# Cross-attention and mixture-of-experts block on one core: the rows are routed without being normalised first

## The chip, the cores and the metric

The kernel runs on one core of one Trainium2 chip. The metric is the device time of one execution in microseconds; the median of three executions is given. The profile is one further execution of the same program, with times counted from the start of its span. Engines are named as in the profile: PE is TensorE, DVE is VectorE, ACT is ScalarE, POOL is GpSimd, SP is SyncE; PEld is TensorE's weight load, and a "q" behind an engine's name (SPq, ACTq) is a DMA that it issues.

## The reference, cut to what matters

```python
# x: (16, 112, 256) = 1792 rows of 256; ctx: (16, 375, 256)
x = x + xattn(layernorm(x), ctx, ctx, mask, Wq, bq, Wk, bk, Wv, bv, Wo, bo)   # 16 heads of 16
x = x + ffn(layernorm(x), router_w, w1, w2)

def ffn(flat, router_w, w1, w2):                  # flat: (1792, 256), router_w: (256, 8)
    gate_probs = softmax(flat @ router_w)
    topk_w, topk_idx = top_k(gate_probs, 2)
    topk_w = topk_w / clip(topk_w.sum(-1), 1e-9)
    cw = zeros(T, 8).at[arange(T)[:, None], topk_idx].add(topk_w)
    h = silu(einsum('td,edf->etf', flat, w1))     # 8 experts, 256 -> 512 -> 256
    y = einsum('etf,efd->etd', h, w2)
    return einsum('etd,te->td', y, cw)
```

`layernorm` takes the mean off a row and divides by the root of its variance plus 1e-5.

## The kernel before

The program has three phases. A prologue loads and transposes x, projects the queries of all 16 batches and fills the first keys and values. Then come 16 turns, one for each batch (`turn(b)`, L1725 on PE): scores and their maxima for the next batch (`head_scores`, the maxima on DVE at L1105), transposed scores (`quad_scores`, L1626), exponentials on ACT (`exps`, L834), outputs (`quad_outputs`, L1640), and the projections of a later batch (`product`, L1546). The third phase is the experts: 21 steps of 256 gathered rows (`step(t)`), from about 299 us to the end.

Between the second and the third lies the routing. The 1792 rows are 14 tiles of 128. `UNITS` (L64) groups them: six units of two tiles and, last, units 6 and 7 of one tile each. For each unit u:

- `project_output(u)` on PE makes the attention's projection, `residual(u)` on DVE (L1231) adds x and the bias and leaves the sum in `x2`;
- `row_vars(u)` on DVE (L1238, L1245, L1247) makes mean and variance, `roots(u)` on POOL (L715) the inverse root, and `normalise_rows(u)` on POOL (L723, units 0 to 5) or `normalise_late(u)` on DVE (L1284, units 6 and 7) writes the normalised rows to `xn2`;
- `write_rows(u)` on SP (L546) copies them to `xn_rows` in DRAM, from which the experts gather them;
- `flat_transpose(u)` on PE (L1709) transposes `xn2` into PSUM, `flat_high(u)` on ACT (L942) copies it out as the high part, `flat_low(u)` on DVE (L1290) makes the low part, and `route(u)` on PE (L1719, L1721) multiplies: a tile takes four matmuls, two for each half of the 256 columns;
- `read_logits(u)` on DVE (L1296) adds the two halves of the result into `logits`.

When the logits of the first eight tiles are there, `find_two(early_tiles, 4)` on DVE (L1315 to L1324) finds the two best experts of each row; `rank_early` on PE counts, `place_rows(0)` on DVE (L1347 to L1353) makes each row's place, ACT makes the one-hot places (`places_in_block`, L972 and L976), POOL and DVE the lanes (L731, L1359). The same follows for the last six tiles (`find_two(late_tiles, 8)`, `rank_late`, L1866 to L1872, `place_rows(1)`, `places_in_block(TOP, ...)`). `fill_lanes` (L1880) and `list_rows` on PE and `list_tokens` on DVE (L1396, L1397) then make the list by which POOL gathers the rows (L765). `gather_rows` waits for that list and for all eight copies to DRAM. PE runs `spin` (L1907), matmuls whose results nobody reads, until the first rows are there.

The order on every engine is written out by hand: an engine runs its list in that order, and a wait holds all that stands behind it. On PE the attention of the last batch and the routing of the first units are interleaved. On SP the two loads of the experts' weights (L552 and L557, 4 MB each) stand between the copies of the rows.

Of the kernel before, what the change touches and what calls it, by code (L numbers as in the profile page):

```python
# [5 lines left out]
F32 = mybir.dt.float32  # L6
F32R = mybir.dt.float32r
# [59 lines left out]
BK_FLAT = (3, 5, 3, 5, 1, 2, 3, 5)  # L67
BK_RANK, BK_LATE, BK_PLACED, BK_TOKEN = 4, 6, 7, 0
# [37 lines left out]
def xattn_moe_kernel(nc, x_rows, x_tiles, ctx_t, mask, wq_t, wk_t, wv_t, wo_t, bq, bk, bv, bo,  # L106
                     router_w, w1, w2, out):
    ctx = ExitStack()
    with ctx:
# [27 lines left out]
        rw = sb("router_parts", [P, KD, 2 * E], F32R)  # L137
# [42 lines left out]
        def expert_buffers(p):  # L180
# [113 lines left out]
        cursor["at"] = last_query_at  # L294
        fh = [sb(f"flat_t_hi{p}", [P, KD, TG], F32R) for p in range(2)]
        fl = [sb(f"flat_t_lo{p}", [P, KD, TG], F32R) for p in range(2)]
# [43 lines left out]
        wh_ready, wl_ready, rw_ready = (sem(n) for n in (  # L340
            "wh_ready", "wl_ready", "rw_ready"))
        ch_ready, cl_ready = (sem(n) for n in ("ch_ready", "cl_ready"))
        keep_in = [sem(f"keep_in{p}") for p in range(2)]
        mask_in, first_low_stacked, masked_set, mask_rows_ready, mask_written = (sem(n) for n in (
            "mask_in", "first_low_stacked", "masked_set", "mask_rows_ready", "mask_written"))
# [22 lines left out]
        ft_done, fh_ready, fl_ready, logits_done = (sem(n) for n in (  # L368
            "ft_done", "fh_ready", "fl_ready", "logits_done"))
# [40 lines left out]
        def stack_part(queue, b, c, src, done):  # L410
            for a in range(2):
# [3 lines left out]
                                src[half:half + P // 2, b.n // 2, b.n % 2, :, :].bitcast(F32)).then_inc(done, 16)  # L415

# [5 lines left out]
        def _(sp):  # L422
# [117 lines left out]
            def write_rows(u):  # L540
                if u < 6:
                    sp.wait_ge(early_xn_ready, u + 1)
                else:
                    sp.wait_ge(late_xn_ready, u - 5)
                tiles = tiles_of(u)
                sp.dma_start(xn_rows[1 + P * tiles.start:1 + P * tiles.stop, :].rearrange("(n p) d -> p n d", p=P),  # L546
                             xn2[u % XN_RINGS][:, 0:UNITS[u][1], :]).then_inc(xn_written[u % XN_RINGS], 16)
# [11 lines left out]
            for u in range(6, 8):  # L559
                write_rows(u)  # L560

# [18 lines left out]
        def _(pool):  # L580
# [26 lines left out]
            def keep_rows():  # L607
                pool.wait_ge(mask_in, 16)
                pool.wait_ge(zeros_set, 1)
                pool.tensor_scalar(masked[:, :], m_all[:, :], 0.0, None, ALU.is_equal).then_inc(masked_set, 1)  # L610
                pool.wait_ge(masked_set, 1)
# [173 lines left out]
        def _(act):  # L785
# [1262 lines left out]
```

## Time and profile before

| what | us |
|---|---|
| median of 3 runs | 452.66 (452.36 to 453.35) |
| the profiled execution, its own time | 451.87 |
| its span | 449.9 |
| PE busy | 411.5 (91%) |
| DVE busy | 336.4 (75%) |
| ACT busy | 279.8 (62%) |
| POOL busy | 223.9 (50%) |
| mean granted TensorE clock | 0.959 of full speed |

The profiled execution lies 0.8 us under the median of the runs. A busy PE is not a PE at its peak, since matmuls overlap: the time that one costs is the distance from its start to the start of the next. The granted clock has two levels, 2.4 GHz (1.00) and 1.2 GHz (0.50).

### The profile page before, as it was taken

What the parts mean: (1) busy time and instruction counts of PE and PEld (TensorE: products, weight loads), DVE (VectorE), ACT (ScalarE), POOL (GpSimd) and SP (SyncE); (2) the same over time, 40 slices, a digit from 0 to 9 for tenths busy, and PEclk for the clock granted to TensorE, in tenths of its full rate; (3) what the DMA queues carried; (4) which work ended last, traced back from release to release, by engine and by line L of the source; (5) the groups of instructions that cost most, each with busy time, mean ns of one, the idle gap of its engine ahead of it and who ended that gap; (6) DMA issues with size and microseconds to landing.
All of it is one profiled execution on the core that took longest, in us unless ns stands there. A gap on an engine that the chain in (4) does not pass through costs nothing.

```text
span 449.9 us, 10827 instructions
## 1 busy us (share of the span) xinstructions
PE 411.5 (91%) x4219; PEld 382.5 (85%) x4219; DVE 336.4 (75%) x700; ACT 279.8 (62%) x381; POOL 223.9 (50%) x257
## 2 busy tenths in 40 slices
PE   7878999999999999999999996899999999999910
PEld 6747898999989999999998985789999999999910
DVE  7866778778877888787788778856886667776536
ACT  4767476665566665766555554648778777778600
POOL 6757443312444223433202764675787878876420
PEclk9999999999999999999999997589999999999975
DMA  7995676768866778766450259822222322332169
GB/s 213 237 199 155 135 158 131 150 150 162 197 159 156 153 140 189 157 132 128 96 120 3 75 205 365 272 68 73 85 80 85 95 83 94 83 82 73 47 231 306
DMA packets 44675, 64.32 MB, mean 143 GB/s; under 512 B 6801, under 2 KB 33570, under 8 KB 44626
## 3 DMA queue, kind: packets, MB, share of 16 engines
q1 hardware_dynamic: 38322, 50.40, 45.6%
q0 software_dynamic: 4096, 11.13, 8.2%
q10 hardware_dynamic: 2208, 2.12, 1.4%
q8 instruction: 33, 0.54, 0.5%
q14 instruction: 16, 0.13, 0.1%
HBM read 30.13 MB, written 9.28 MB: 88 GB/s over the span
## 4 chain that ended last, share of the span: by engine, by line
PE 79%; DVE 9%; DMA 5%; ACT 3%; issue 2%; POOL 1%; ACTq 0%; SPq 0%; DVEq 0%
PE ps L1546 41%; PE ps L1609 12%; PE ps L1626 9%; PE ps L1640 9%; PE ps L1915 2%; DVE x L1536 2%; PE ps L1653 2%; DMA q_stack<-attn_t_lo 1%; DMA y_back<-y_rows 1%; DVE neg_max L1105 1%; DMA keep<-keep_scratch 1%; PE ps L1709 1%; DMA keep_scratch<-keep_all 1%; PE ps L1665 1%; PE ps L1719 1%
## 5 line engine op out<-in xcount | busy, mean ns | idle before, releaser
L1105 DVE TENSOR_REDUCE neg_max<-ps 112x1 f32<-112x376 f32 x256 | 133.6, 545 | 41.4 <-PE ps L1609 36.5
L834 ACT ACTIVATE probs<-ps 125x1344 f32<-125x1344 f32 x64 | 82.8, 1294 | 43.4 <-PE ps L1626 38.2
L1609 PE MATMUL ps<-k_stack,q_stack 98*112 98x376 f32 x256 | 86.2, 369 | 3.7 <-DVE neg_max L1105 2.2
L604 POOL TENSOR_TENSOR k_lo<-k_f,k_hi 128x752 fp32r<-128x752 f32 x16 | 28.9, 1806 | 112.3 <-ACT k_hi L808 111.8
L765 POOL DMA_INDIRECT rows<-xn_rows,token_of_row x42 | 55.8, 1328 | 17.5 <-issue 12.5
L773 POOL DMA_INDIRECT y_rows<-y_out,slot_of_row x42 | 45.6, 1087 | 25.3 <-ACT y_out L1027 14.4
L1609 PEld LDWEIGHTS ps<-k_stack,q_stack 98*112 98x112 f32 x256 | 44.1, 174 | 16.3 <-DVE neg_max L1105 10.9
L1626 PE MATMUL ps<-q_stack,k_stack 100*125 100x224 f32 x384 | 52.6, 273 | 0.0
L1626 PEld LDWEIGHTS ps<-q_stack,k_stack 100*125 100x125 f32 x384 | 50.4, 188 | 0.7 <-ACT probs L834 0.5
L1546 PE MATMUL ps<-w_hi,h_hi 128*128 128x256 f32 x168 | 48.8, 290 | 0.4 <-DVE h_lo L1452 0.4
L1546 PE MATMUL ps<-flat_t_hi,w_hi 128*128 128x256 f32 x168 | 47.5, 283 | 1.3 <-DVE flat_t_lo L1430 1.3
L1546 PE MATMUL ps<-flat_t_hi,w_lo 128*128 128x256 f32 x168 | 47.2, 281 | 0.0
L1546 PE MATMUL ps<-flat_t_lo,w_hi 128*128 128x256 f32 x168 | 47.2, 281 | 0.0
L1546 PE MATMUL ps<-w_hi,h_lo 128*128 128x256 f32 x168 | 47.0, 280 | 0.0
L1546 PE MATMUL ps<-w_lo,h_hi 128*128 128x256 f32 x168 | 47.0, 280 | 0.0
L1640 PE MATMUL ps<-probs,v_wide 125*32 125x112 f32 x1536 | 47.0, 262 | 0.0
L1640 PEld LDWEIGHTS ps<-probs,v_wide 125*32 125x32 f32 x1536 | 35.1, 109 | 8.0 <-issue 5.7
L1008 ACT ACTIVATE h_f<-ps 128x1024 f32<-128x1024 f32 x21 | 21.6, 1026 | 24.3 <-PE ps L1546 24.3
L1546 PEld LDWEIGHTS ps<-flat_t_hi,w_hi 128*128 128x128 f32 x168 | 31.9, 190 | 1.7 <-DVE flat_t_lo L1430 1.7
L1546 PEld LDWEIGHTS ps<-w_hi,h_hi 128*128 128x128 f32 x168 | 31.9, 190 | 0.9 <-DVE h_lo L1452 0.9
L1452 DVE TENSOR_TENSOR h_lo<-h_f,h_hi 128x1024 fp32r<-128x1024 f32 x21 | 25.7, 1225 | 8.9 <-ACT h_hi L1013 8.9
L1546 PEld LDWEIGHTS ps<-w_lo,h_hi 128*128 128x128 f32 x168 | 31.9, 190 | 0.0
(213 smaller groups left out, 1017.6 us busy)
## 6 DMA issues: line engine op xcount, KB each, us to landing
k_stack<-k_hi SPq DMA_DIRECT2D x32, 376.0 KB, 5.0
w_all<-w SPq DMA_DIRECT2D x2, 4096.0 KB, 18.8
k_stack<-k_lo SPq DMA_DIRECT2D x16, 376.0 KB, 5.5
ctx_raw<-ctx_t SPq DMA_DIRECT2D x32, 187.5 KB, 3.9
q_stack<-attn_t_hi SPq DMA_DIRECT2D x64, 56.0 KB
y_back<-y_rows SPq DMA_DIRECT2D x14, 256.0 KB, 5.1
x_rows_sb<-x_rows SPq DMA_DIRECT2D x4, 448.0 KB, 4.6
x<-x_tiles SPq DMA_DIRECT2D x7, 256.0 KB, 2.9
```

The source lines that it names most:

```text
L604: pool.tensor_tensor(kl[:, :, :], kf[:, :, :], kh[:, :, :].bitcast(F32), ALU.subtract)\
L765: pool.indirect_dma_start(rows[t.ring][:, a, :], None, xn_rows, row_of(token_i, t, a))\
L773: pool.indirect_dma_start(y_rows, row_of(slot_i, t, a), yo[t.par][:, a, :], None)\
L834: act.activation(pf[j % 2][:, :, :], ps[0:CT, BK_ST:BK_ST + KT, 0:4 * S], ACT.Exp).then_inc(pf_ready, 1)
L1008: act.activation(hf[t.par][:, :, :], silu_source(t), ACT.Silu).then_inc(hf_ready, 1)
L1105: dve.tensor_reduce(neg_max[:, head:head + 1], ps[0:S, BK_MAX + s % 2, 0:CP], AX.X, ALU.max, negate=True).then_inc(max_read, 1)
L1452: dve.tensor_tensor(hl[t.par][:, :, :], hf[t.par][:, :, :], hh[t.par][:, :, :].bitcast(F32), ALU.subtract).then_inc(hl_ready, 1)
L1536: dve.scalar_tensor_tensor(out=x2[:, n, :], in0=y_back[:, c, n, :], scalar=weight[:, c, n:n + 1], in1=x2[:, n, :], op0=ALU.mult, op1=ALU.add)\
L1546: last = pe.matmul(o, lhs, rhs, start=first and n == 0, stop=final and n == len(terms) - 1)
L1609: pe.matmul(ps[0:S, BK_MAX + a, 0:CP], qs[b.ring][0:R_MAX, a, q, :], ks[b.ring][0:R_MAX, q, :], start=True, stop=True).then_inc(smax_done, 1)
L1626: last = pe.matmul(ps[0:CT, BK_ST + k3, 2 * S * q:2 * S * (q + 1)], ks[b.ring][0:ROWS, 2 * j + q, k3 * CT:(k3 + 1) * CT], qs[b.ring][0:ROW ...
L1640: last = pe.matmul(ps[VC * i:VC * (i + 1), BK_OUT, S * j:S * (j + 1)], vx[b.par][:, k3, 2 * j + i // 2 + HALF * (i % 2), :], pf[j % 2][:, ...
```

## The change

The rows are transposed and routed as they stand in `x2`, behind their residual, without mean and root taken off. To make up for the mean, the router's columns are centred once: PE multiplies the router by a matrix of 1/256 (`mean_of`), which gives each column's mean on all partitions, ACT copies it to `router_mean`, and POOL takes it off the router. This happens in the second turn. The root comes in where the gates are made: `below_maximum` multiplies by `row_rstd`, one step more. The transposed rows leave PSUM once, in fp32 (`copy_flat`), and a tile is routed by two fp32 products. `flat_high`, `flat_low` and the router's two parts are gone. PE's, DVE's and ACT's orders around the last batch are written anew, and the copies of units 6 and 7 to DRAM are issued by ACT instead of SP.

```diff
@@ SP @@
-            for u in range(6, 8):
-                write_rows(u)
@@ POOL, in the loop over the turns @@
+            def centre_router():
+                pool.wait_ge(mean_copied, 1)
+                pool.wait_ge(rw_in, 16)
+                pool.tensor_tensor(rw_raw[:, :, :], rw_raw[:, :, :], router_mean[:, :].rearrange("p (a e) -> p a e", a=1)
+                                   .to_broadcast([P, KD, E]), ALU.subtract).then_inc(router_ready, 1)
+
             for b in range(B + 1):
                 turn(Batch(0, b))
+                if b == 0:
+                    pool.memset(mean_of[:, :], 1.0 / D).then_inc(router_ready, 1)
+                if b == 2:
+                    centre_router()
@@ ACT @@
             def out_copy(b):
                 act.wait_ge(pv_done, QUADS * (b.n + 1))
+                if b.n == 1:
+                    act.wait_ge(mean_done, 1)
+                    act.copy(router_mean[:, :], ps[:, BK_OUT, SUMS:SUMS + E]).then_inc(mean_copied, 1)
...
-            act.wait_ge(rw_in, 16)
-            act.copy(rw[:, :, 0:E], rw_raw[:, :, :]).then_inc(rw_ready, 1)
...
-                act.copy(fh[u % 2][:, :, 0:n], ps[:, BK_FLAT[u], 0:KD * n].rearrange("p (k n) -> p k n", k=KD))\
-                    .then_inc(fh_ready, 1)
+                act.copy(flat_t[u % 2][:, :, 0:n], ps[:, BK_FLAT[u], 0:KD * n].rearrange("p (k n) -> p k n", k=KD))\
+                    .then_inc(flat_ready, 1)
...
-            flat_high(0)
+            copy_flat(0)
             exps(last, 0)
-            flat_high(1)
             out_copy(last.after(-1))
             exps(last, 1)
+            copy_flat(1)
             attn_high(last.after(-1))
-            flat_high(2)
             exps(last, 2)
             exps(last, 3)
+            copy_flat(2)
             out_copy(last)
-            flat_high(3)
-            flat_high(4)
+            copy_flat(3)
+            copy_flat(4)
             attn_high(last)
-            for u in range(5, len(UNITS)):
-                flat_high(u)
+            copy_flat(5)
+
+            def write_late_rows(u):
+                act.wait_ge(late_xn_ready, u - 5)
+                store_rows(act, u)
+
+            write_late_rows(6)
+            copy_flat(6)
+            copy_flat(7)
...
             for k, c in enumerate((1, 0)):
                 places_in_block(k, c, slice(0, EARLY_NT))
+            write_late_rows(7)
             places_in_block(TOP, 1, slice(EARLY_NT, NT))
@@ DVE @@
-                dve.tensor_reduce(logits[:, tiles_of(u), :], ps[:, BK_FLAT[u], 0:2 * E * UNITS[u][1]]
-                                  .rearrange("p (n h e) -> p n e h", h=2, e=E), AX.X, ALU.add).then_inc(logits_read, 1)
+                dve.tensor_copy(logits[:, tiles_of(u), :], ps[:, BK_FLAT[u], 0:E * UNITS[u][1]]
+                                .rearrange("p (n e) -> p n e", e=E)).then_inc(logits_read, 1)
...
-                dve.tensor_tensor(shifted[:, :, :], logits[:, :, :], wide2(c0), ALU.subtract).then_inc(shifted_ready, 1)
+                step(dve.tensor_tensor(t0[:, :, :], logits[:, :, :], wide2(c0), ALU.subtract))
+                dve.wait_ge(row_rstd_ready, len(UNITS))
+                dve.tensor_tensor(shifted[:, :, :], t0[:, :, :], wide2(row_rstd), ALU.mult).then_inc(shifted_ready, 1)
...
             row_vars(2)
-            flat_low(0)
             residual(4)
             row_vars(3)
             read_logits(0)
             normalise(last.after(-1))
+            row_vars(4)
             attn_low(last.after(-1))
-            row_vars(4)
             residual(5)
-            flat_low(1)
+            read_logits(1)
             row_vars(5)
             residual(6)
-            read_logits(1)
+            read_logits(2)
+            normalise(last)
             row_vars(6)
-            flat_low(2)
             normalise_late(6)
-            normalise(last)
-            flat_low(3)
-            read_logits(2)
-            flat_low(4)
+            read_logits(3)
             attn_low(last)
-            read_logits(3)
             find_two(early_tiles, 4)
             residual(7)
             row_vars(7)
-            flat_low(5)
-            flat_low(6)
+            place_rows(0, early_tiles, BK_RANK)
+            read_logits(4)
             normalise_late(7)
-            place_rows(0, early_tiles, BK_RANK)
-            flat_low(7)
-            read_logits(4)
             read_logits(5)
@@ PE, flat_transpose, route, the second turn and the order of the last batch @@
-                if u < 6:
-                    pe.wait_ge(early_xn_ready, u + 1)
-                else:
-                    pe.wait_ge(late_xn_ready, u - 5)
+                pe.wait_ge(resid_added, u + 1)
...
-                    for k in range(KD):
-                        pe.matmul(ps[:, BK_FLAT[u], 2 * E * a:2 * E * (a + 1)], fh[u % 2][:, k, m], rw[:, k, :],
-                                  start=k == 0, stop=False)
-                        last = pe.matmul(ps[:, BK_FLAT[u], 2 * E * a:2 * E * a + E], fl[u % 2][:, k, m],
-                                         rw[:, k, 0:E], start=False, stop=k == KD - 1)
+                    last = product(ps[:, BK_FLAT[u], E * a:E * (a + 1)],
+                                   [(flat_t[u % 2][:, k, m], rw_raw[:, k, :]) for k in range(KD)])
...
                 outputs(b, 1)
+                if b.n == 1:
+                    pe.wait_ge(router_ready, 1)
+                    pe.wait_ge(rw_in, 16)
+                    product(ps[:, BK_OUT, SUMS:SUMS + E], [(mean_of[:, :], rw_raw[:, k, :]) for k in range(KD)])\
+                        .then_inc(mean_done, 1)
...
             quad_outputs(before, 2)
             flat_transpose(0)
+            quad_scores(last, 0)
             project_output(4)
-            quad_scores(last, 0)
             quad_outputs(before, 3)
-            flat_transpose(1)
             route(0)
             quad_scores(last, 1)
             out_transpose(before)
             quad_outputs(last, 0)
-            flat_transpose(2)
+            flat_transpose(1)
+            quad_scores(last, 2)
             attn_transpose(before)
-            quad_scores(last, 2)
             project_output(5)
             quad_outputs(last, 1)
             quad_scores(last, 3)
+            route(1)
+            flat_transpose(2)
+            quad_outputs(last, 2)
             project_output(6)
-            quad_outputs(last, 2)
-            route(1)
             quad_outputs(last, 3)
+            route(2)
             flat_transpose(3)
+            out_transpose(last)
+            route(3)
+            attn_transpose(last)
             flat_transpose(4)
-            out_transpose(last)
-            route(2)
-            attn_transpose(last)
-            route(3)
             flat_transpose(5)
             route(4)
             project_output(7)
+            rank_early()
             flat_transpose(6)
-            rank_early()
             route(5)
```

## Rows read from the trace of the kernel before

**Rows 1.** The page: the chain that ended last, by engine.

```profile
PE 79%; DVE 9%; DMA 5%; ACT 3%; issue 2%; POOL 1%; ACTq 0%; SPq 0%; DVEq 0%
```

**Rows 2.** Busy time in stretches: us, then each engine (xinstructions), granted clock, DMA.

```profile
76.00:91.00 15.00, 15.00 (x185) 13.77 (x183) 11.99 (x27) 9.22 (x13) 3.56 (x2) 1.00 0.78 166
...
250.00:260.00 10.00, 10.00 (x160) 9.05 (x159) 5.89 (x22) 6.93 (x12) 7.42 (x7) 1.00 0.25 84
...
275.00:280.00 5.00, 3.47 (x18) 3.29 (x18) 4.01 (x18) 2.76 (x10) 3.15 (x5) 0.61 1.06 375
```

**Rows 3.** The chain that ended last, from the last batch's first scores: start, us.

```profile
251.55 0.59 PE ps L1709 x4
252.14 1.43 PE ps L1546 x12
253.58 0.65 PE ps L1626 x6
...
255.54 0.11 PE ps L1721
...
268.75 0.69 DVE flat_t_lo L1290
```

**Rows 4.** SP's DMA issues by time, and how long the maxima's copies took to land.

```profile
250.41 1.46 SPq L467 DMA_DIRECT2D q_stack<-max_rows  x2
...
DMA to landing us min/median/max: 2.1/2.2/2.2
...
264.75 4.73 SPq L546 DMA_DIRECT2D xn_rows<-xn  x2
269.52 0.89 SPq L557 DMA_DIRECT2D w_all<-w  x1
270.46 15.51 SPq L546 DMA_DIRECT2D xn_rows<-xn  x2
```

**Rows 5.** Forms by line: duration in ns min/median/max, first and last start.

```profile
L1719 PE MATMUL ps<-router_parts,flat_t_hi x28: 256/256/381, 255.3 to 278.5; 128*128 128x16 f32 x28
...
L1792 PEld LDWEIGHTS ps<-ident x32: 192/333/338, 1.7 to 7.4; 128*128 128x128 f32 x32
```

**Rows 6.** PE by time, [idle before, and what ended it].

```profile
268.06 0.41 PE L1665 MATMUL ps<-ident,attn_rows 112*128 112x112 f32 x2
...
272.63 0.27 PE L1850 MATMUL ps<-both_experts,earlier 128*128 128x64 f32 x1 [0.59 <-DVE both_experts L1319]
...
275.36 0.28 PE L1719 MATMUL ps<-router_parts,flat_t_hi 128*128 128x16 f32 x1 [1.37 <-DVE flat_t_lo L1290]
...
278.09 0.38 PE L1719 MATMUL ps<-router_parts,flat_t_hi 128*128 128x16 f32 x1 [0.27 <-DVE flat_t_lo L1290]
```

**Rows 7.** DVE by time.

```profile
270.12 0.69 DVE L1315 TENSOR_TENSOR ahead<-gate 128x512 f32<-128x512 f32 x1
...
273.42 0.42 DVE L1231 TENSOR_TENSOR x<-ps,x 128x256 f32<-128x256 f32 x1
...
274.63 1.01 DVE L1290 TENSOR_TENSOR flat_t_lo<-ps,flat_t_hi 128x512 fp32r<-128x512 f32 x2
...
277.14 0.17 DVE L1353 SCALAR_TENSOR_TENSOR in_block<-lane_of,place 128x16 f32<-128x16 f32 x1
...
279.35 0.56 DVE L1315 TENSOR_TENSOR ahead<-gate 128x384 f32<-128x384 f32 x1
...
291.05 0.29 DVE L1391 CAST lane_tokens<-ps 112x128 fp32r<-112x128 f32 x1 [0.33 <-PE ps L1880]
```

**Rows 8.** ACT by time.

```profile
268.61 0.61 ACT L827 ACTIVATE attn_t_hi<-ps,bv_c 128x112 fp32r<-128x112 f32 x2
...
277.47 2.44 ACT L972 ACTIVATE is_place<-numbers,in_block 128x128 fp32r<-128x128 f32 x8
...
285.72 1.86 ACT L972 ACTIVATE is_place<-numbers,in_block 128x128 fp32r<-128x128 f32 x6 [1.29 <-DVE in_block L1353]
```

**Rows 9.** POOL by time.

```profile
266.67 2.42 POOL L723 TENSOR_SCALAR xn<-x,moments,row_rstd 128x256 f32<-128x256 f32 x2
```

More of the change, by code:

```diff
@@ L67 @@
 BK_FLAT = (3, 5, 3, 5, 1, 2, 3, 5)
+SUMS = QUADS * S
 BK_RANK, BK_LATE, BK_PLACED, BK_TOKEN = 4, 6, 7, 0
@@ L294, in xattn_moe_kernel @@
         cursor["at"] = last_query_at
+        mean_of = sb("mean_of", [P, P])
+        router_mean = sb("router_mean", [P, E])
+        cursor["at"] = last_query_at
         fh = [sb(f"flat_t_hi{p}", [P, KD, TG], F32R) for p in range(2)]
+        cursor["at"] = last_query_at
+        flat_t = [sb(f"flat_t{p}", [P, KD, TG]) for p in range(2)]
         fl = [sb(f"flat_t_lo{p}", [P, KD, TG], F32R) for p in range(2)]
@@ L339, in xattn_moe_kernel @@
             "zeros_set", "const_set", "ident_set", "filled"))
-        wh_ready, wl_ready, rw_ready = (sem(n) for n in (
-            "wh_ready", "wl_ready", "rw_ready"))
+        wh_ready, wl_ready, router_ready = (sem(n) for n in (
+            "wh_ready", "wl_ready", "router_ready"))
         ch_ready, cl_ready = (sem(n) for n in ("ch_ready", "cl_ready"))
         keep_in = [sem(f"keep_in{p}") for p in range(2)]
-        mask_in, first_low_stacked, masked_set, mask_rows_ready, mask_written = (sem(n) for n in (
-            "mask_in", "first_low_stacked", "masked_set", "mask_rows_ready", "mask_written"))
+        mask_in, first_low_stacked, mask_rows_ready, mask_written = (sem(n) for n in (
+            "mask_in", "first_low_stacked", "mask_rows_ready", "mask_written"))
         kproj_done, kf_ready, kh_ready, kl_ready = (sem(n) for n in (
@@ L367, in xattn_moe_kernel @@
             "power_set", "row_var_ready", "row_rstd_ready", "early_xn_ready", "late_xn_ready"))
-        ft_done, fh_ready, fl_ready, logits_done = (sem(n) for n in (
-            "ft_done", "fh_ready", "fl_ready", "logits_done"))
+        ft_done, flat_ready, mean_done, mean_copied, logits_done = (sem(n) for n in (
+            "ft_done", "flat_ready", "mean_done", "mean_copied", "logits_done"))
         logits_read, shifted_ready, gate_exp = (sem(n) for n in (
@@ L415, in stack_part, with store_rows @@
                                 src[half:half + P // 2, b.n // 2, b.n % 2, :, :].bitcast(F32)).then_inc(done, 16)
+        def store_rows(queue, u):
+            tiles = tiles_of(u)
+            queue.dma_start(xn_rows[1 + P * tiles.start:1 + P * tiles.stop, :].rearrange("(n p) d -> p n d", p=P),
+                            xn2[u % XN_RINGS][:, 0:UNITS[u][1], :]).then_inc(xn_written[u % XN_RINGS], 16)
         def pairs(x):
@@ L540, in write_rows @@
             def write_rows(u):
-                if u < 6:
-                    sp.wait_ge(early_xn_ready, u + 1)
-                else:
[L544 to L547, printed above, removed]
+                sp.wait_ge(early_xn_ready, u + 1)
+                store_rows(sp, u)
             for u in range(0, 4):
@@ L609, in keep_rows @@
                 pool.wait_ge(zeros_set, 1)
[L610 to L611 removed]
+                pool.tensor_scalar(masked[:, :], m_all[:, :], 0.0, None, ALU.is_equal).then_inc(zeros_set, 1)
+                pool.wait_ge(zeros_set, 2)
                 pool.tensor_scalar(keep_all[:, :], masked[:, :], -1.0, 1.0, ALU.mult, ALU.add)\
@@ L935, in turn, with copy_flat @@
                     exps(b, 3)
-            def flat_high(u):
+            def copy_flat(u):
                 act.wait_ge(ft_done, u + 1)
@@ L1708, in flat_transpose @@
                         at = P * (n * k + a)
-                        last = pe.transpose(ps[:, BK_FLAT[u], at:at + P], xn2[u % XN_RINGS][:, a, k * P:(k + 1) * P],
+                        last = pe.transpose(ps[:, BK_FLAT[u], at:at + P], x2[:, tiles_of(u).start + a, k * P:(k + 1) * P],
                                             ident[:, :])
```

17 lines of the change are left out of this document (3 added, 14 removed).

## The prediction

> **What bounds the kernel now.** I read the page's chain first. It is 79% PE [rows 1]. The stretches then say where that holds: a turn's 15 us have PE busy for all 15.00, and so has 250 to 260 [rows 2]. In the turns and in the first half of the routing, what is added to PE is paid in full. From about 268 on PE has holes, and DVE and ACT set the pace: the chain goes through `flat_low` and the steps of `find_two` [rows 3]. Read the rows of PE, DVE and ACT side by side there [rows 6, 7, 8]: the last attention transpose at 268.06, `find_two` early at 270.12, places in block known at 277.14 plus 0.17, `find_two` late at 279.35, ACT's late places at 285.72 and the lanes' sum read at 291.05. Behind this last one everything up to the first expert step hangs on the list, so I take a shift of the list to be the shift of the end.
>
> **What it removes.** DVE loses eight `flat_low`. A two-tile one costs 0.6, start to start, of a duration of 0.69 [rows 3]; five, six and seven are 0.93 and 0.35 more (two of them stand as 1.01, [rows 7]). Before 268 these lie in DVE's idle time (DVE is busy 5.89 of 10 in 250 to 260, [rows 2]) and are worth nothing. On the path lie those between the last transpose and 279.35. POOL's `normalise_rows`, 2.42 for two tiles [rows 9], no longer stands ahead of a transpose; before 268 PE never waited for it (PE 10.00 of 10, [rows 2]), so that is worth nothing either. PE's count stays: four fp32r matmuls a tile go, and two fp32 products come, each of which the trace runs as two instructions (L1792 is 16 products and has x32, [rows 5]). Their weight load takes 192 ns at full clock, and routing steps by 0.11 us a matmul [rows 3, 5]: 0.9 for two tiles, before and after. Bounds: 0.06 a matmul if the eight columns hid half of it, 0.21 at half clock, so between -0.4 and +0.8 for a unit on the path. I take the equal price, because the load is of the same shape. The prologue's two router copies lie in slack.
>
> **What it adds early.** Two products with `mean_of` in the second turn are four instructions, 4 x 0.11 = **+0.45** on a PE with no idle time there [rows 2]; bounds 0.1 (they slip under the outputs' tail) and 0.85 (half clock, 0.21 each). ACT's copy, POOL's two instructions and the memset lie beside them: ACT is busy 9.22 of 15 and POOL 3.56 [rows 2]. The further step of `below_maximum`, about 0.3, fits into DVE's 0.33 of idle time ahead of the lanes' sum [rows 7]; without that cover it would cost its 0.3.
>
> **What it moves, on PE.** The new order puts `quad_scores(last, 0)` directly behind `flat_transpose(0)`, at 252.1. It waits for the maxima's copies. SP issues these from 250.41 on, the second at about 251.0, and they land 2.1 to 2.2 later [rows 4]: 253.2. Before, `project_output(4)`'s 1.43 filled the gap and the scores came at 253.58 [rows 3]. Now PE stands idle for **1.1**. Behind it stand the projection, so the residual of unit 4, and all the last batch. Further on `route(3)` moves ahead of the last attention transpose (+0.9), one unit's transposes go behind it (-0.45), and `route(3)` must itself wait for its transposes' copy on ACT, with only `out_transpose` between (about +0.3). The attention transpose thus goes from 268.06 to 268.06 + 1.1 + 0.9 - 0.45 + 0.3 = 269.9.
>
> **On ACT and DVE.** `attn_high` then waits behind `copy_flat(4)`, whose transposes now come behind the attention transpose: 269.9 + 0.15 + 0.5 (transposes) + 0.55 (copy) = 271.1, and 0.61 for itself [rows 8]. `attn_low` is done 0.7 later, and `find_two` early starts at 272.5 instead of 270.12: **+2.4**. From there DVE runs without a gap: 3.30 for `find_two` (270.12 to 273.42), 1.2 for residual and variances (273.42 to 274.63, [rows 7]), then directly 1.43 for places, and 0.1 + 0.45 + 0.1 + 0.5 + 0.1 + 0.3 for reading, `normalise_late` and counting, 7.5 in all, against 9.23 before (270.12 to 279.35). `find_two` late starts at 280.0: 2.4 - 1.75 = **+0.65**. Places in block for the early tiles come at 278.4 instead of 277.3, ACT's seven microseconds of early places end at 285.5 instead of 284.4, and its late ones, at 285.72 before with 1.29 to spare [rows 8], still wait for DVE.
>
> PE's own branch competes with that: `rank_early` now stands ahead of `flat_transpose(6)` and waits for `find_two` until 274.9. At full clock units 5 to 7 are routed by 278.7, well in time. But the granted clock falls in that stretch: its mean is 0.61 over 275 to 280 [rows 2], which is 1.1 us at 2.4 GHz and the rest at 1.2, so it fell at 276.1, after PE had stood idle for 0.59 and 1.37 [rows 6]. With the same date, unit 5 takes 1.7, units 6 and 7 0.9 each with their transposes between, and the last logits are read at 280.4: `find_two` late at 280.6, **+1.25**. The new order leaves a hole of the same kind (273.1 to 274.9), so I take a value between, **+1.0**.
>
> **The copies to DRAM.** SP's two issues behind the second weight load took 15.51 together, nearly all of it the first [rows 4], which cost nothing on SP. Now ACT issues them, and behind unit 6's stand `copy_flat(6)`, the route of unit 6 and all places. Unit 6's comes at 272.3; SP issues the second weight load only after unit 5's copy, which waits for 2.42 of POOL behind the same variances, at about 274. So ACT is first, and pays some 0.45. Unit 7's comes at 285.5, about when the old stall ended (270.46 + 15.0). It has 0.9 to 1.2 of slack before ACT's late places.
>
> The Trainium skill (Perfetto Trace Analysis, "DMA Instruction — HWDGE (DVE, Sync)") says that the descriptor generator is one block, locked for exclusive use until all descriptors of a DMA are made, shared by the two queues. The rows agree as far as they go: an issue behind a 4 MB load is held. By that rule ACT could be held like SP; whether it is, the trace before can't show. By the order above the rule would cost the forecast under 0.5, and its worse form is a rival.
>
> **Sum.** 0.45 + 1.0 = +1.45 on a profiled execution of 451.87: 453.3. The median of the runs stands 0.8 higher, so **454.1** there. Its own range: 452.66 + 0.1 + 0.5 = 453.3 up to 452.66 + 0.85 + 2.5 = 456.0, where 2.5 is the case of a clock that falls already in the new hole, at about 273: `rank_early` then ends 1.1 later and routing is at half pace throughout.
>
> **Rivals.**
> - *DVE's relief goes through: faster.* If the last attention transpose stays within 0.5 of 268.06, because the scores don't wait for the copies or later slack swallows it, the 1.75 taken off DVE remain: 452.66 + 0.45 - 1.75 = 451.35. It decides at a shift of `find_two` early of 1.3: below that the kernel is faster. For it: DVE has idle time in 250 to 260 to catch up. Against it: PE has none. 13%.
> - *It comes out even.* PE's loss of 1.1 is half won back, for example as the first exponentials run earlier and ACT no longer delays the outputs: +0.45 - 0.25 = 452.9. 25%.
> - *The clock falls sooner*, in the hole at 273, in most executions: 455.5 to 456. 5%.
> - *ACT is held by the descriptor generator*, by the rule above, if the second weight load gets ahead of unit 6's copy: released at about 286.3, routing of units 6 and 7 ends at 288, ACT's late places start 8.5 later: 461.5. Against it is the order of waits worked out above. 4%.
> - The rest, 53%, is my forecast.
>
> **Numbers.** A measurement of this kernel can tell about 0.2%, 0.9 us, from no change. Slower: the forecast and the last two rivals, 62% (its lower edge lies inside the 0.9, the even case's upper edge outside, and I let these cancel). Same: the even case, 25%. Faster: 13%. The range of 8 in 10 reaches to the faster rival and to the early clock: 451.4 to 456.2.
>
> **What would show it.** PE idle for about 1 us before the first `quad_scores` of the last batch, its releaser the maxima's DMA; the last attention transpose near 270; `find_two` early near 272.5 and late at 280 to 280.6 (less the 0.45 of the second turn, which shifts all dates); ACT's DMA issues of about 0.4 each. I am wrong if the first is missing, if the fp32 products take other than 0.11 an instruction, or if ACT's issue lasts microseconds.

## The result: slower, by nearly three times what was forecast

The changed kernel took 456.74 us (455.72 to 457.28, four runs) against 452.55 (452.36 to 453.35, four runs) of the kernel before: a ratio of 1.0087, 95% interval 1.0065 to 1.0108. A second measurement of the same two gave 456.34 against 452.46, 1.0086 (1.0059 to 1.0113). The forecast was 454.1, its range 451.4 to 456.2. The sign was right, the size was not: about +4 us for +1.45.

The profiled execution of the changed kernel took 455.72 us, its span is 453.4, its mean granted clock 0.946 (before 451.87, 449.9 and 0.959). The page's chain by engine and the granted clock in 40 slices, to be read against [rows 1]:

```profile
PEclk9989999999999999999999995589999999999975
PE 80%; DVE 8%; DMA 6%; ACT 2%; issue 2%; POOL 1%; ACTq 0%; SPq 0%; DVEq 0%
```

The same stretches as in [rows 2]:

```profile
76.00:91.00 15.00, 15.00 (x185) 13.84 (x184) 12.16 (x26) 9.74 (x12) 3.80 (x4) 1.00 0.77 155
250.00:260.00 10.00, 8.95 (x149) 7.87 (x147) 5.57 (x20) 5.11 (x7) 6.74 (x7) 1.00 0.25 83
275.00:280.00 5.00, 4.88 (x22) 4.48 (x22) 4.31 (x15) 0.37 (x1) 0.56 (x1) 0.50 1.05 374
```

A turn still has PE busy throughout. In 250 to 260 PE, full before, now idles for 1.05. In 275 to 280 it is the other way round: PE was busy 3.47 of 5 and is now at 4.88, at half clock all the time; ACT was busy 2.76 and is now at 0.37. The list of rows has moved from VectorE and ScalarE over to TensorE.

The chain in order of time shows the wait that was forecast:

```profile
251.46 0.27 DVE max_rows L1138
...
252.00 2.20 DMA q_stack<-max_rows
...
254.24 0.91 PE ps L1631 x6
```

PE by time, for [rows 6]:

```profile
254.24 0.91 PE L1631 MATMUL ps<-q_stack,k_stack 100*125 100x224 f32 x6 [1.05 <-DMA q_stack<-max_rows]
...
271.32 0.39 PE L1670 MATMUL ps<-ident,attn_rows 112*128 112x112 f32 x2
271.54 1.84 PE L1711 MATMUL ps<-ident,x 128*128 128x128 f32 x8
...
276.68 0.40 PE L1856 MATMUL ps<-both_experts,earlier 128*128 128x64 f32 x1
...
279.35 1.71 PE L1551 MATMUL ps<-router_raw,flat_t 128*128 128x8 f32 x8
...
285.38 0.41 PE L1872 MATMUL ps<-both_early,ones 128*128 128x56 f32 x1 [2.29 <-DVE both_experts L1330]
```

DVE by time, for [rows 7]:

```profile
251.16 0.26 DVE L1136 CAST max_rows<-ps 16x112 fp32r<-16x112 f32 x1
...
274.18 0.68 DVE L1326 TENSOR_TENSOR ahead<-gate 128x512 f32<-128x512 f32 x1
...
280.32 0.18 DVE L1366 SCALAR_TENSOR_TENSOR in_block<-lane_of,place 128x16 f32<-128x16 f32 x1
...
282.27 0.17 DVE L1307 COPY gate<-ps 128x8 f32<-128x8 f32 x1 [0.62 <-PE ps L1551]
283.12 0.17 DVE L1307 COPY gate<-ps 128x8 f32<-128x8 f32 x1 [0.69 <-PE ps L1551]
283.33 0.56 DVE L1326 TENSOR_TENSOR ahead<-gate 128x384 f32<-128x384 f32 x1
...
294.46 0.28 DVE L1342 TENSOR_TENSOR gate<-gate,row_rstd 128x112 f32<-128x112 f32 x1
294.73 0.29 DVE L1404 CAST lane_tokens<-ps 112x128 fp32r<-112x128 f32 x1
```

ACT by time, with its DMA issues, for [rows 8]:

```profile
273.42 0.36 ACTq L425 DMA_DIRECT2D xn_rows<-xn  x1
...
287.79 0.35 ACTq L425 DMA_DIRECT2D xn_rows<-xn  x1
289.41 1.86 ACT L993 ACTIVATE is_place<-numbers,in_block 128x128 fp32r<-128x128 f32 x6 [0.57 <-DVE in_block L1366]
```

`find_two` early starts 4.06 later than in [rows 7], `find_two` late 3.98, the read of the lanes' sum 3.68, the first gather of rows 3.69 (296.83 against 293.14). Two waits of 0.62 and 0.69 stand ahead of `find_two` late, and both are for routes on TensorE: here DVE does not set the pace any more.

### The profile page after: what moved, and what is told of

Same layout as the page of the kernel before. It is cut to its first block, busy times and chain, and to the rows that moved or that the text cites. A ratio compares the mean times of both kernels' runs of the same rounds, so it can differ in the third digit from the quotient of the medians.

```text
span 453.4 us, 10833 instructions
## 1 busy us (share of the span) xinstructions
PE 415.8 (92%) x4223; PEld 387.0 (85%) x4223; DVE 332.3 (73%) x692; ACT 279.8 (62%) x381; POOL 224.6 (50%) x259
## 4 chain that ended last, share of the span: by engine, by line
PE 80%; DVE 8%; DMA 6%; ACT 2%; issue 2%; POOL 1%; ACTq 0%; SPq 0%; DVEq 0%
PE ps L1551 43%; PE ps L1614 12%; PE ps L1631 9%; PE ps L1645 9%; DVE x L1541 2%; PE ps L1921 2%; PE ps L1658 1%; DMA q_stack<-attn_t_lo 1%; DMA y_back<-y_rows 1%; DVE neg_max L1127 1%; PE ps L1711 1%; DMA keep_scratch<-keep_all 1%; DMA keep<-keep_scratch 1%; PE ps L1670 1%; DMA mask_all<-mask 1%
## 5 line engine op out<-in xcount | busy, mean ns | idle before, releaser
L1551 PEld LDWEIGHTS ps<-flat_t_hi,w_lo 128*128 128x128 f32 x168 | 31.9, 190 | 0.0
```

Of the source, the lines that this page charges most:

```text
L1551: last = pe.matmul(o, lhs, rhs, start=first and n == 0, stop=final and n == len(terms) - 1)
```

## The experiments

The table uses a few milestones, read from the one trace of each kernel. *Maxima* is the first cast of the last batch's maxima on DVE (250.11 before, 251.16 changed), *early* and *late* are the starts of `find_two`, *gather* is POOL's first gather of rows, and *fall* is where the granted clock goes from 2.4 to 1.2 GHz, from stretches of 2 to 3 us. The ratio is of the medians of all executions, and a trace is one of them: that of e11 took 455.13, the longest of its twelve. From the first gather to the last scatter of outputs all 17 traces take 138.1 to 138.5, so the first gather carries a shift over to the end, as the forecast assumed. Times in us:

| kernel | ratio to before (95%) | maxima to early | early to late | fall | maxima to gather |
|---|---|---|---|---|---|
| before | 1 | 20.01 | 9.23 | 276.1 | 43.03 |
| changed | 1.0087 (1.0065 to 1.0108) | 23.02 | 9.15 | 271.6 | 45.67 |
| e0 changed again | 1.0086 (1.0059 to 1.0113) | 22.63 | 9.24 | 275.8 | 45.39 |
| e1 orders of before | 0.9991 (0.9968 to 1.0015) | 19.88 | 8.47 | 274.4 | 42.07 |
| e2 scores back | 1.0047 (1.0024 to 1.0070) | 21.68 | 9.14 | 270.4 | 44.35 |
| e3 no mean | 1.0053 (1.0029 to 1.0077) | 22.87 | 9.24 | 275.4 | 45.63 |
| e4 wide routes | 1.0047 (1.0029 to 1.0066) | 22.80 | 8.09 | 278.5 | 43.96 |
| e5 before, filled | 1.0028 (0.9998 to 1.0057) | 20.21 | 11.81 | 272.0 | 45.13 |
| e6 e1, filled | 0.9994 (0.9975 to 1.0013) | 19.90 | 8.49 | 276.6 | 42.32 |
| e7 mean in the gap | 1.0068 (1.0045 to 1.0090) | 23.39 | 9.14 | 271.2 | 46.05 |
| e8 route(5) first | 1.0065 (1.0045 to 1.0085) | 22.42 | 8.62 | 273.8 | 44.85 |
| e9 best order | 0.9998 (0.9978 to 1.0017) | 19.89 | 9.13 | 271.7 | 42.99 |
| e10 e9, half the mean | 0.9979 (0.9956 to 1.0002) | 19.89 | 7.39 | 274.3 | 41.06 |
| e11 attention first | 1.0012 (0.9993 to 1.0030) | 20.80 | 9.40 | 271.8 | 43.72 |
| e12 e10, wide | 0.9996 (0.9981 to 1.0011) | 20.10 | 7.02 | 277.5 | 41.41 |
| e13 e1, wide | 1.0008 (0.9998 to 1.0018) | 20.09 | 7.82 | 280.8 | 41.87 |
| e14 before, wide | 1.0001 (0.9990 to 1.0012) | 20.05 | 9.90 | 273.8 | 43.54 |

**e0, the changed kernel again.**

> The changed kernel itself, unedited, beside the runs of the same call and with more executions of both kernels. If the first comparison (456.74 against 452.55) holds, its ratio lies in 1.0065 to 1.0108; if four executions were too few, nearer to the 1.0032 that was forecast.

The loss is real, and the trace speaks against my first theory. From the changed kernel's first trace I had blamed the clock: it fell 4.5 us sooner than before. The stretch of the fall, in the first trace and in this one:

```profile
270.00:272.00 2.00, 1.76 (x15) 1.60 (x14) 1.35 (x5) 0.35 (x1) 0.26 (x1) 0.90 1.04 391
```

```profile
274.00:276.00 2.00, 0.88 (x6) 0.68 (x6) 1.91 (x3) 0.00 (x0) 0.66 (x1) 0.96 1.05 389
276.00:278.00 2.00, 1.65 (x7) 1.55 (x7) 1.82 (x7) 0.00 (x0) 0.00 (x0) 0.50 1.03 343
```

A mean of 0.90 in two microseconds is 1.6 at full and 0.4 at half clock: down at 271.6. Here it is down at 275.8, about the date of before, and the gather comes only 0.28 sooner from the maxima. PE of this trace says why:

```profile
276.35 0.39 PE L1856 MATMUL ps<-both_experts,earlier 128*128 128x64 f32 x1 [1.47 <-DVE both_experts L1330]
...
277.02 1.66 PE L1862 MATMUL ps<-both_experts,ones 128*128 128x56 f32 x7
```

`rank_early` starts at 276.35, behind either date. It and what stands behind it, the transposes of units 6 and 7 and the routes of units 5 to 7, run at half clock in both, and last to 282.75: 6.4 us. The executions without a trace agree that the clock does not set the two kernels apart: the mean granted clock of the whole kernel is 0.946 to 0.951 in the six of the changed kernel and 0.943 to 0.959 in the 25 of the kernel before, with medians of 0.950 both.

**e1, the orders of before.** PE's, DVE's and ACT's lists from `flat_transpose(0)` on as before, with the new arithmetic; ACT still issues the copies of units 6 and 7. PE's list, cut:

```diff
-            quad_scores(last, 0)
             project_output(4)
+            quad_scores(last, 0)
             quad_outputs(before, 3)
+            flat_transpose(1)
             route(0)
...
-            rank_early()
             flat_transpose(6)
+            rank_early()
             route(5)
```

> The changed kernel's arithmetic with the orders of TensorE, VectorE and ScalarE as they were before the change. Theory A (the loss is the clock's earlier fall, brought on by the thin fp32 routes that stand before it, wherever they stand): the clock still falls before 273, find_two early ends its wait later than in the kernel before, and the time is within 1 us of the changed kernel's 456.7. Theory B (the loss is the new order: scores ahead of the projection, and the 1.05 us wait): that wait is gone, the clock falls at 275 or later, and the time is 453.5 to 455.

Theory A is out. B was right in direction and claimed too little: the median is 452.53, under its 453.5 to 455, and the whole loss goes, though the clock fell at 274.4 and not at 275 or later. The maxima to early distance is 19.88, that of before within 0.13, with 24 fp32 route instructions in place of 24 fp32r ones ahead of the last attention transpose: the prices are equal. Of DVE's relief 0.76 comes through. Its timeline shows what holds the rest:

```profile
271.37 0.69 DVE L1326 TENSOR_TENSOR ahead<-gate 128x512 f32<-128x512 f32 x1
...
276.65 0.41 DVE L1302 TENSOR_SCALAR xn<-x,moments,row_rstd 128x256 f32<-128x256 f32 x1 [0.68 <-POOL row_rstd L718]
...
279.64 0.17 DVE L1307 COPY gate<-ps 128x8 f32<-128x8 f32 x1 [0.54 <-PE ps L1551]
279.84 0.56 DVE L1326 TENSOR_TENSOR ahead<-gate 128x384 f32<-128x384 f32 x1
```

**e2, scores back behind the projection.**

```diff
-            quad_scores(last, 0)
             project_output(4)
+            quad_scores(last, 0)
```

> The changed kernel with project_output(4) ahead of the last batch's first scores again, as before the change. The 1.05 us that TensorE waited for the maxima's copies should go under the projection's 1.07 us of work. If that wait is on the path to the end, the time falls by 0.8 to 1.1 us against the changed kernel (455.6 to 455.9); if the clock's date decides alone and stays, the same; if the clock falls earlier still because the hole is gone and the thin work comes sooner, no gain at all or a loss.

From `flat_transpose(0)` to the outputs behind it PE takes 2.71 from start to start (252.53 to 255.24), against 3.98 in the changed kernel (252.54 to 256.52). The wait is written as 1.05 and costs 1.3; that the matmuls ahead of it no longer overlap those behind it would fit, and no run isolates it. The ratio falls by 0.0039, 1.8 us; with the half widths of the two intervals added in squares that is 0.2 to 3.4. The trace says 1.0 to 1.3 at the gather.

**e3 and e7, the mean of the router.** Of e3, which drops ACT's copy and POOL's centring with it, so that the router is multiplied uncentred, and of e7, which has the copy and the centring later too:

```diff
-                if b.n == 1:
-                    pe.wait_ge(router_ready, 1)
-                    pe.wait_ge(rw_in, 16)
-                    product(ps[:, BK_OUT, SUMS:SUMS + E], [(mean_of[:, :], rw_raw[:, k, :]) for k in range(KD)])\
-                        .then_inc(mean_done, 1)
```

```diff
             flat_transpose(0)
+            pe.wait_ge(router_ready, 1)
+            pe.wait_ge(rw_in, 16)
+            product(ps[:, 6, 0:E], [(mean_of[:, :], rw_raw[:, k, :]) for k in range(KD)])\
+                .then_inc(mean_done, 1)
             quad_scores(last, 0)
```

> The changed kernel without the mean product, its copy and the centring on GpSimd: left out is the centring of the router, which is multiplied uncentred. Theory of the forecast: the four fp32 products in the second turn cost 0.45 to 0.65 us of TensorE there and nothing else, so the time falls by 0.5 to 0.7 (456.0 to 456.2). If the whole early shift of 1.05 us (to the last batch's maxima) hangs on it, 455.7. If some later slack takes it in, no change.

> The changed kernel with the mean product, its copy and the centring moved from the second turn into the gap in which TensorE waits for the maxima's copies (behind flat_transpose(0)), in another bank. The four instructions then lie in the wait. If what they cost in the second turn is real, the last batch's maxima come 0.65 us earlier there and the time falls by 0.5 to 1.0 against the changed kernel; if the gap is not free (route(0) now waits for the centring, about 257.0 against 257.2), nothing is won.

From one turn's maxima to the next it is 13.75 before and 14.40 in the changed kernel in that turn; 13.72 in e3 and 13.73 in e7. So the four instructions cost **0.65**, not 0.45. In e3 this is all that changes up to the gather (maxima to gather 45.63); its ratio is 0.0033 lower, 1.5 us, more than the 0.65 explains and within what the two intervals leave. In e7 the maxima come 0.72 sooner than in e0, but only 0.35 of it is left at the first scores (253.85 against 254.20), and at the gather 0.06: the issue of the maxima's two copies took 1.90 on SP in place of 1.53, and PE waited for them 1.08 all the same. The gap gives 0.65 back only if the copies come. The measured 0.8 us by ratio is not explained by this trace, and the two intervals leave it anything from -0.8 to 2.4.

**e4, wide routes.** The same eight columns of the router sixteen times over.

```diff
-                    last = product(ps[:, BK_FLAT[u], E * a:E * (a + 1)],
-                                   [(flat_t[u % 2][:, k, m], rw_raw[:, k, :]) for k in range(KD)])
+                    last = product(ps[:, BK_FLAT[u], P * a:P * (a + 1)].rearrange("p (w e) -> p w e", e=E),
+                                   [(flat_t[u % 2][:, k, m], rw_raw[:, k:k + 1, :].to_broadcast([P, P // E, E]))
+                                    for k in range(KD)])
```

> The changed kernel with the routes' moving operand read 16 times over, 128 columns in place of 8; the other 120 results are not read. Theory A (the clock falls early because the thin routes keep TensorE's array nearly idle although its queue is busy): the fall moves from 271.6 to 275 or later, or goes away, and the time comes to 453.5 to 455.5 although each route takes as long or longer. Theory C (the fall's date follows from the length of the stretch, not from what the products hold): the fall stays at 271 to 272 and the time is 456.7 or more (up to 458 if 128 columns cost more than 8).

Theory A's numbers hold here (278.5, and 1.8 us less by ratio). Read with e0, not any later fall helps, but one behind 277: at 275.8 early to late stayed at 9.24, and at 278.5 it is 8.09, as `rank_early` runs at full clock (its seven matmuls take 0.94 for 1.66). DVE still waits 0.61 for the last route. 128 columns cost 0.1 more for eight instructions than 8 do.

**e8, route(5) ahead of rank_early** in the changed kernel.

```diff
+            route(5)
             rank_early()
             flat_transpose(6)
-            route(5)
```

> The changed kernel with route(5) ahead of rank_early. Its two tiles then fall into the hole in which TensorE waits 1.47 us for find_two (at full clock 0.9, at half 1.7). Theory E (find_two late is held by TensorE's own list behind rank_early: rank, transposes and routes of units 5 to 7 at half pace): find_two late comes 0.8 to 1.7 us sooner behind find_two early (7.6 to 8.4 in place of 9.24) and the time falls by as much, to 454.7 to 455.6. Theory D (VectorE or ScalarE hold it): no change in that distance, 456.4.

Early to late falls by 0.62, the lower edge missed by 0.2; the time, 456.11, missed its 454.7 to 455.6, and 1.0065 is not told from e0's 1.0086. The clock fell at 273.8 and the route ran at half pace, so the hole was too short for it:

```profile
275.71 1.71 PE L1551 MATMUL ps<-router_raw,flat_t 128*128 128x8 f32 x8
277.27 0.40 PE L1856 MATMUL ps<-both_experts,earlier 128*128 128x64 f32 x1
```

**e11, the attention transpose first.** e2, and in PE's list the last attention transpose ahead of `route(3)`:

```diff
-            route(2)
             flat_transpose(3)
             out_transpose(last)
-            route(3)
+            route(2)
             attn_transpose(last)
+            route(3)
             flat_transpose(4)
```

> The changed kernel with project_output(4) ahead of the first scores again, the last attention transpose ahead of route(3) (route(2) fills the wait behind out_transpose), and ScalarE's and VectorE's lists to match. By the forecast's terms (1.3 for the wait, 0.9 + 0.24 for route(3), 0.5 for the copy ahead of attn_high) find_two early comes 2.0 to 2.8 us sooner, at about 271.3, and the time falls to 453.6 to 454.4. What is still missing against before is then behind find_two early, in TensorE's list.

Maxima to early is 20.80, 1.8 to 2.2 less than in the changed kernel. By e2 the wait gives 1.0 to 1.3 of it, the attention transpose and `attn_high` ahead of `copy_flat(4)` another 0.9. What is left at early to late is 9.40, against 8.47 with the lists of before. The median of 453.82 came as expected, `find_two` early (271.93, not 271.3) did not quite. By ratio it is 3.3 us less than e0, at the gather 1.7: one trace does not show the rest.

**e5 and e6, filling TensorE's holes.** 36 matmuls of 256 columns whose results are not used; e5 is the kernel before with them, e6 is e1 with them.

```diff
             flat_transpose(6)
+            fill_time(4, BK_PLACED, True)
             rank_early()
+            fill_time(10, BK_PLACED)
             route(5)
...
+            fill_time(18, BK_PLACED)
             rank_late()
+            fill_time(4, BK_SPIN)
             fill_lanes(0)
```

> The kernel before with 36 matmuls of 256 columns into a bank that is rewritten later, 4, 10, 18 and 4 of them in the holes of TensorE ahead of rank_early, of route(5), of rank_late and of the lanes' fill. Theory A (the low clock of 276 to 297 is what holds the stretch): the granted clock stays at 2.4 GHz through it or falls much later, and the time falls by 1 to 2 us, to 451 to 452. Theory D (VectorE and ScalarE hold the stretch and the clock costs little): the same time within 0.5 us, whatever the clock does. If the matmuls themselves get in the way, slower by up to 1 us.

> The changed kernel's arithmetic in the orders of before, with the same 36 matmuls in TensorE's holes. The orders alone gave 0.9991 of before. If the clock then stays high, VectorE's relief should come through: 452.5 less 1 to 2 us, 450.5 to 451.5, and find_two late at most 7.5 us behind find_two early in place of 8.47. If VectorE and ScalarE hold the stretch anyway, no change.

In e5's trace they backfired. The clock fell at 272.0, before the first of them (272.76), and ten matmuls stood in the way of `route(5)` for 2.5 us. DVE then waited 2.86 for the copy of unit 7's transposes, which stand behind that route, and 0.35 for the last route:

```profile
275.81 2.48 PE L1866 MATMUL ps<-earlier,ones 128*128 128x256 f32 x10
278.09 0.21 PE L1719 MATMUL ps<-router_parts,flat_t_hi 128*128 128x16 f32 x1
```

The ratio of e5 does not tell it from the kernel before, as its executions go both ways with the clock: the five with a mean of 0.962 or more took 451.2 to 452.9, the seven with 0.958 or less 453.6 to 456.9, the kernel before beside them 452.46. In e6 the clock was low for 13.7 us instead of e1's 20.5, and nothing came of it: DVE keeps e1's two waits, 0.69 and 0.55, early to late is 8.49 where 7.5 was expected, and the time, 451.96, is above its 450.5 to 451.5.

**e9, e10, e12, e13, e14: is it the lists or the clock's date?** e9 takes the orders of before and is to remove DVE's two waits:

```diff
             flat_transpose(6)
+            route(5)
             rank_early()
-            route(5)
-            flat_transpose(7)
             route(6)
+            flat_transpose(7)
...
-            normalise_late(7)
             place_rows(0, early_tiles, BK_RANK)
+            normalise_late(7)
```

e10 adds the router's two halves on POOL first, so that the mean is one product. e12 is e10 and e13 is e1 with e4's edit; e14 is the kernel before with 8 copies of its 16 columns.

```diff
                     pool.memset(mean_of[:, :], 1.0 / D)
+                    pool.wait_ge(rw_in, 16)
+                    pool.tensor_tensor(router_sum[:, :], rw_raw[:, 0, :], rw_raw[:, 1, :], ALU.add)\
...
-                    product(ps[:, BK_OUT, SUMS:SUMS + E], [(mean_of[:, :], rw_raw[:, k, :]) for k in range(KD)])\
+                    product(ps[:, BK_OUT, SUMS:SUMS + E], [(mean_of[:, :], router_sum[:, :])])\
```

> The changed arithmetic in the orders of before, with route(5) ahead of rank_early, route(6) ahead of flat_transpose(7), and unit 7's normalisation on VectorE behind the early places. The orders of before alone gave 0.9991. Theory E: VectorE's two waits of that stretch, 0.68 for GpSimd's root and 0.54 for the last route, go away, the distance between the two find_two falls from 8.47 to 7.3, and the time is 0.7 to 1.2 us under that of before (ratio 0.9973 to 0.9985); ScalarE's early places (7.0 us) can take the last 0.4 of it back. Theory D: no change, 0.999.

> e9 with the two halves of the router added on GpSimd first, so that the second turn has one fp32 product (two instructions) in place of two (four). If the instructions cost what they take, half of the 0.65 us comes back: 0.3 us less than e9. If it is the stop of TensorE's stream that costs, nothing comes back.

> e10 with the routes' moving operand read 16 times over (128 columns). e9 and e10 have the same lists behind the last attention transpose, and yet find_two late stood 9.13 us behind find_two early in the one, where the clock fell at 271.7, and 7.39 in the other, where it fell at 274.3. If the date of the fall decides, and the wide routes put it off as they did in e4 (278.5), the distance is 7.4 to 7.8 in nearly all executions, and the time is 0.5 to 1.5 us under e10: ratio 0.994 to 0.997. If the date doesn't decide, or 128 columns cost more than they give, 0.998 to 1.002.

> The changed arithmetic in the orders of before (e1, ratio 0.9991) with the wide routes. Here route(5) still stands behind rank_early. If the date of the fall decides in this order too: find_two late 7.5 to 7.9 behind find_two early in place of 8.47, ratio 0.996 to 0.998. If the waits for GpSimd's root and the last route are what is left, as in the filled kernel (8.49 with half the low clock), 0.999 to 1.000.

> The kernel before with its routes' moving operands read over to 128 columns (8 copies of 16, and of the first 8 of each). VectorE holds the stretch there (no wait of over 0.3 us between the two find_two), so a later fall of the clock should give little: ratio 0.998 to 1.000. If the low clock costs the kernel before as much as the changed one, 0.995 to 0.997.

e9 and e10 are the cleanest pair: the same lists around the whole last batch, and a difference only in the second turn. e9 itself missed what was expected, 7.3 and 0.9973 to 0.9985, with 9.13 and 0.9998. PE and DVE of e9:

```profile
273.28 1.72 PE L1551 MATMUL ps<-router_raw,flat_t 128*128 128x8 f32 x8
...
280.29 0.71 DVE L1326 TENSOR_TENSOR ahead<-gate 128x384 f32<-128x384 f32 x1
```

and of e10:

```profile
272.46 0.96 PE L1555 MATMUL ps<-router_raw,flat_t 128*128 128x8 f32 x8
...
278.44 0.56 DVE L1330 TENSOR_TENSOR ahead<-gate 128x384 f32<-128x384 f32 x1
```

With the clock down at 271.7 the route fills the hole and more, and early to late is 9.13; with 274.3 it fits, and the distance is 7.39, where the forecast had 7.5. e12 reaches 7.02, below its 7.4 to 7.8, and e13 7.82. With one trace each, the four distances fit one account: the list must let TensorE be done early, and the clock must hold until it is. The times did not follow: e12 and e13 were forecast at 0.994 to 0.998 and gave 0.9996 and 1.0008. ACT of e12 shows one place where the gain is given back:

```profile
281.11 2.44 ACT L997 ACTIVATE is_place<-numbers,in_block 128x128 fp32r<-128x128 f32 x8 [0.56 <-DMA xn_rows<-xn]
```

The early places lie where the normalised rows of units 3 to 5 lay, so ACT waits until their copies to DRAM have landed. The last of them, unit 5's, is issued by SP just ahead of the second weight load:

```profile
269.99 0.36 SPq L426 DMA_DIRECT2D xn_rows<-xn  x1
270.39 2.27 SPq L564 DMA_DIRECT2D w_all<-w  x1
```

It lands 11.0 us after its issue, at 281.0. In e10 the same copy took 10.6, and ACT waited 0.27. Unit 6's copy, issued by ACT at 270.75, landed after 6.2, and nothing waited for it. Behind this, PE fills the lanes at half clock and DVE waits 0.43 for it. The rest, from the last scatter to the end, is 17.6 to 19.9 in the traces whatever the kernel, and hides a microsecond either way.

Widening did not put off the fall in the kernel before: in e14 it came at 273.8, against 276.1 in that kernel's own trace and 272.0 in e5, which is that kernel up to there. So e14 does not test a later fall. With the earlier one the time is the same (1.0001) and the distance longer, 9.90 for 9.23.

One product for two took 14.17 and 14.16 for the turn (e10, e12) where two took 14.40. No version beats the kernel before by what can be told; e10 comes nearest, at 1.1% under the changed kernel (0.9979 against 1.0087).

## Why the prediction was wrong

- **The mean product, +0.45: mis-sized.** It is 0.65 for four instructions and 0.42 for two. Two points give 0.115 an instruction and 0.19 once, an estimate; that the 0.19 is for breaking the stream is not shown. The changed trace:

```profile
70.24 0.61 PE L1551 MATMUL ps<-router_raw,mean_of 128*128 128x8 f32 x4
```

- **A shift of 0.46 that the forecast did not have.** The first maxima come at 39.06 in the changed kernel against 38.58, but at 39.04 in e5 and at 38.72 in e14 too, which are the kernel before up to there. In 26 to 28 the granted clock was 1.00 in the trace of the kernel before, 0.50 in the changed one and 0.55 in e5. So most of it can be execution. The 14 traces with the new arithmetic all lie at 38.80 to 39.69, so that some tenths of it may still be the change's; no run settles that.
- **PE's wait for the copies, 1.1: right**, with its releaser. Its price was 1.3.
- **The attention transpose: right in mechanism.** From the maxima it moved by 2.21, where the terms 1.1 + 0.9 - 0.45 + 0.3 give 1.85. `route(3)`'s wait for ACT is written as 0.24. `find_two` early was to move by 2.4, and moved by 2.62 (e0) and 3.01 (the clock was already low, the transposes behind took 1.84 for 1.04).
- **Equal price of the routes, the extra step of `below_maximum` hidden, ACT's DMA issues not held: right.** Equal price by e1, where 24 of each kind take the same time within 0.13. Late to gather shrank, 13.79 to 13.50, though the step of 0.28 was added (294.46). ACT's issues took 0.36 and 0.35. In e12 one of them fell at 270.75 into SP's issue of the second weight load (270.39, 2.27 long) and took 0.36, and the other, at 283.59, took 0.34 in the 15 us behind such a load for which SP's next issue was held before the change. So the rival by the Trainium skill's rule (Perfetto Trace Analysis, "DMA Instruction — HWDGE (DVE, Sync)") that one generator is locked for both queues is not borne out here for ACT's issues.
- **The step that failed** is the regain behind `find_two` early, cut short too little for TensorE's own list: "With the same date, unit 5 takes 1.7, units 6 and 7 0.9 each", `find_two` late at 280.6, **+1.25**, "I take a value between, **+1.0**". From the maxima, late moved by 2.93 and in e0 by 2.63. The regain of 1.75 was counted in before it was asked what TensorE would still have to do: `rank_early` now stands ahead of the transposes of units 6 and 7 and of the routes of units 5 to 7, and waits for a `find_two` that itself comes 2.4 later. I had the first 1.2 us of that list (274.9 to 276.1) ahead of the fall; with the shifts it starts at 276.68, and in e0 at 276.35, behind the fall in both traces (271.6 and 275.8), and takes 6.4 for my 5.5. Of the regain of 1.75 nothing was left: early to late is 9.15 and 9.24, against 9.23 before. e9, e10 and e12 point to both, its order and its pace. DVE's own 7.5 was 0.5 too long (7.02 in e12, where no wait of DVE is listed between the two), and it was bound by TensorE all the same.
- I had this outcome in hand, with another trigger (a fall at about 273, which e0 does without), as the upper end of my own range ("`rank_early` then ends 1.1 later and routing is at half pace throughout", +2.5) and as a rival at 5%. 0.65 + 2.5 gives 455.8 by the medians; 456.3 to 456.7 was measured.
- **The account:** 0.65 + 2.6 to 3.0 (early) + 0 (no regain) - 0.3 (late to gather) = 2.9 to 3.4 at the gather, of 2.7 to 5.1 by the intervals' ratio. Some 0.5 to 1.3 us of the medians' 3.9 to 4.2 stays open. A part of it may be the shift ahead of the first maxima, and the end of the kernel varies by more than that from trace to trace.

## What to carry to other kernels

Work taken off an engine is a gain only as far as the next one lets it: before booking a regain, write down the list of every other engine for the same stretch, from the new start dates, and see which ends last. If TensorE's clock falls in the stretch, do this with the fall on both sides of the list's start; here the regain was lost as soon as the list stood behind the fall, and 271.6 or 275.8 made no difference to it. And an exchange of two lines that leaves a transfer uncovered costs more than its idle row says (1.3 for 1.05).

## What was not expected of the hardware

- **The clock fell without a hole before it.** In the changed kernel it went down at 271.6, where PE had been busy for 5.00 of 260 to 265 and 3.00 of 265 to 268, with 0.24 of idle time behind that. With the new arithmetic and 8 columns it fell between 270.4 and 276.6, and 271.6 and 275.8 are one kernel twice. With the wide routes it fell at 277.5 to 280.8 in three of three kernels of that arithmetic, for 0.1 us more in eight instructions. In the arithmetic of before the same widening did not do it (e14, 273.8). The runs don't tell by what rule. The Trainium skill (TensorE: Matmul & The Clock Gate, "What's actually happening") has the gate set by how busy the engine has been recently; PE's busy rows alone would not have told this fall.
- **The width of an fp32 product hardly counts.** Eight instructions of 8 columns take 0.96 to 1.06, of 128 columns 1.06 to 1.16.
- **A transfer beside a weight load lands late.** In e12 the copy issued 0.4 us ahead of the load of 4 MB landed after 11.0 us, where the copies at 252 to 262 in the changed kernel landed after 2.1 to 2.5.
- **Matmuls that fill a hole are no cover once the clock is down:** ten took 1.44 in e6 and 2.48 in e5.
